# The down product of a fused block: token tiles grouped 2, 3, 3 in place of 3, 3, 2

## The chip, the cores and the metric

One core of one Trainium2 chip runs one program. The metric is the device time of one execution, in microseconds (us). The kernel before takes 1655.97 us, the median of three runs (1651.63 to 1657.54).

## What is computed

The reference applies three residual blocks to x, 1024 tokens (16 x 64) of 1024 features: cross attention against a context of 1601 positions, a gated feed-forward block whose hidden values are thinned by rank, and a routed low-rank layer with 8 experts of rank 16. The second block is the one that matters here:

```python
s = silu(x @ w_gate.T)                      # 1024 x 2752
s[the 1376 smallest of |s| in each row] = 0
x = x + (s * (x @ w_up.T)) @ w_down.T        # x is normalised before both products
```

## The kernel before

The program runs attention (`attention_fast`), the feed-forward block (`ffn_fast`, lines 997 to 1602), the routed layer (`mixture`) and a check, each behind a barrier of all engines. The change lies in `ffn_fast`.

The 1024 tokens are eight tiles of 128 tokens. Weights and activations of a product are split in a high and a low part, and each product is the sum of three matmuls (high by high, high by low, low by high). `ffn_fast` computes the gate product into DRAM (`s`), then the up product, transposed, into DRAM (`u_t`). Beside the up product VectorE (DVE) and ScalarE (ACT) search the threshold of each row, tile by tile, and DVE writes the thinned rows to DRAM (`sk`). Four tiles are thinned by then. The thinning of tiles 4 to 7 is interleaved with the down product, by step number: `FINISH_AT = {0: 4, 4: 5, 24: 6, 28: 7}` starts the last four passes of a tile (`nearest`, `best`, `choose`, `keep`, L1358 to L1391) in four steps one after another, and from step 9 (`LATE_ROUNDS_AT`) every second step up to 21 has one round of the search for tiles 6 and 7 (`search`, L1321 to L1350; `compare` on ACT). On the SP queue `LATE_SK_AT = {5: 4, 9: 5, 28: 6, 32: 7}` names the step at which a thinned tile is stored and the row data of the next one is loaded.

The down product takes the tokens in three groups (`GROUPS`), since three tiles by 1024 output features fill six PSUM banks and the transposes need the other two. For each group it runs over the 2752 hidden values in 22 chunks of 128 (the last has 64), so there are 66 steps, n = 0 to 65, and w_down is read and split anew for each group. A step n, for a group of m tiles, is:

- SP: `load_down(n + 2)` waits until POOL is done with the low part of n, and loads a 128 x 1024 chunk of w_down (L1179). `load_turn(n + 3)` then loads m tiles of `sk` (L1169) and of `u_t` (L1172). SP takes these, the stores of thinned tiles and the loads for them in one order.
- GpSimd (POOL): `d_hi` (a cast, L1277) once the matmuls of n - 2 are done, then `d_lo` (L1279). Their size does not depend on m.
- TensorE (PE): `turn(n + 2)`, m transposes (L1578), then `down(n)`, m x 3 x 2 matmuls of 128x512 (L1595).
- DVE: `multiply(n)` (L1416), m x 128 wide, reads the transposes; `take_low(n - 1)` (L1425), as wide, reads two SBUF tiles; then whatever thinning the step has. ACT makes `h_hi` (L1507) between the two.

At the third step of a group DVE adds x to the finished output of the group before (`add_in`, L1433, two operations for each tile). The first product of a group waits for these, tile by tile. At the fourth step SP stores those tiles (L1190), waits for the stores to land, and loads the x of the group now being computed (L1185). The last group's `add_in` and stores stand at the end.

```python
for i in range(len(GROUPS[gi])):
    for a, (hp, wp) in enumerate(((h_hi, d_hi), (h_hi, d_lo), (h_lo, d_hi))):
        for o in range(2):
            last = pe.matmul(bank[2 * i + o][:, :], ...)
```

Of the kernel before, what the change touches and what calls it, by code (L numbers as in the profile page):

```python
# [629 lines left out]
def attention_fast(nc, x, ctx_nat, ctx_t, mask, x1, outside):  # L630
# [3 lines left out]
    with ExitStack() as ctx:  # L634
# [6 lines left out]
        PER = TC  # L641
        GROUPS = B * PER
        UNITS = 2 * B
# [106 lines left out]
        def _(pool):  # L750
            identity(pool, eye[:, :], eye_ready)
            pool.memset(ones[:, :], 1.0).then_inc(ones_ready, 1)
            for g in range(GROUPS):
                if g % PER == LAST:
# [9 lines left out]
        def _(dve):  # L764
# [35 lines left out]
            def add_mask(g, hp):  # L800
                p = g % PER
                h = 2 * g + hp
                r = rows(p)
                if hp == 0:
                    dve.wait_ge(scores_ready, g + 1)
                if h >= SLOTS:
                    dve.wait_ge(exp_done, h + 1 - SLOTS)
                c0, c1 = (c for _, c in parts(p))
                if p == LAST:
                    m = mask_t[0:r, c0].rearrange("p k s -> p (k s)").unsqueeze(1).broadcast_to([r, 4, 256])  # L810
                    into = masked[0:r, h % SLOTS, :].rearrange("p (n q) -> p n q", n=4)
                    of = scores[0:r, h % SLOTS].rearrange("p h (c q) -> p (h c) q", c=2)
                else:
                    m = mask_t[0:r, c0:c1 + 1].rearrange("p c k s -> p (c k s)").unsqueeze(1).broadcast_to([r, 2, 512])
                    into = masked[0:r, h % SLOTS, :].rearrange("p (h n) -> p h n", h=2)
                    of = scores[0:r, h % SLOTS]
                dve.tensor_tensor(into, of, m, ALU.add).then_inc(mask_added, 1)  # L817
# [18 lines left out]

            for g in range(GROUPS + 8):
                if g < GROUPS:
                    add_mask(g, 0)
# [19 lines left out]
        def _(act):  # L859
# [11 lines left out]
            def exponential(g, hp):  # L871
                p = g % PER
                h = 2 * g + hp
                r = rows(p)
                act.wait_ge(mask_added, h + 1)
                if g >= RING and hp == 0:
                    act.wait_ge(pv_done, g + 1 - RING)
                    act.wait_ge(paired, pairs_before(g + 1 - RING))
                act.activation(probs[0:r, g % RING, hp * HALF:(hp + 1) * HALF], masked[0:r, h % SLOTS, :],  # L879
                               ACT.Exp).then_inc(exp_done, 1)  # L880
# [7 lines left out]
            act.wait_ge(mask_turned, 1)  # L888
            for g in range(GROUPS + 4):
                if g < GROUPS:  # L890
                    exponential(g, 0)
# [103 lines left out]
def ffn_fast(nc, x1, w_gate, w_up_t, w_down, s, sk, u_t, x2, settled):  # L995
# [3 lines left out]
    with ExitStack() as ctx:  # L999
# [2 lines left out]
        START, SLOPE, WINDOW = 0.755, 5.3e-4, 4  # L1002
        AIM = float(KEEP_OUT + WINDOW - 1)
        PAIRS = TILES // 2
        GROUPS = ((0, 1, 2), (3, 4, 5), (6, 7))
        STEPS = len(GROUPS) * IC
        MAGS, TURNS, HS, OUTS = 3, 4, 3, 4
        GBANKS = 6
# [1347 lines left out]
def program(nc, x, ctx_nat, ctx_t, mask, w_gate, w_up, w_up_t, w_down, router_wt, router_b, a_t, b_t, out):  # L2356
    qstack = nc.dram_tensor("qstack", [B, 3 * HD, NH * S], F32, kind="Internal").ap()
    shifts = nc.dram_tensor("shifts", [2, 2, HALF_Q], F32, kind="Internal").ap()
    x1 = nc.dram_tensor("x1", [TOK, D], F32, kind="Internal").ap()
    x2 = nc.dram_tensor("x2", [TOK, D], F32, kind="Internal").ap()  # L2360
    s = nc.dram_tensor("s", [TOK, I], F32, kind="Internal").ap()
    u = nc.dram_tensor("u", [TOK, I], F32, kind="Internal").ap()
    sk = nc.dram_tensor("sk", [TOK, I], F32, kind="Internal").ap()
    u_t = nc.dram_tensor("u_t", [I, TOK], F32, kind="Internal").ap()
    with nc.sbuf_tensor("outside", [P, 1], F32) as outside, nc.sbuf_tensor("settled", [P, TILES], F32) as settled, \
            nc.sbuf_tensor("all_bad", [HD, 1], I32) as all_bad:
        attention_fast(nc, x, ctx_nat, ctx_t, mask, x1, outside[:, :])
        ffn_fast(nc, x1, w_gate, w_up_t, w_down, s, sk, u_t, x2, settled)
        mixture(nc, "mix", x2, router_wt, router_b, a_t, b_t, out)
        verdict(nc, outside[:, :], settled[:, :], all_bad[:, :])  # L2370
        bad = nc.values_load(all_bad[0:1, 0:1], min_val=0, max_val=4 * P)
        with nc.If(bad > 0):
            anew(nc, x, ctx_nat, ctx_t, mask, w_gate, w_up, w_down, router_wt, router_b, a_t, b_t, out,
                 qstack, shifts, x1, x2, s, u)
# [36 lines left out]
```

## Time and profile before

| what | value |
|---|---|
| median of three runs | 1655.97 us |
| the profiled execution | 1656.46 us |
| its span, first to last instruction | 1654.8 us |
| PE busy | 1418.1 us (86%) |
| DVE busy | 1052.4 us (64%) |
| POOL busy | 856.0 us (52%) |
| mean granted TensorE clock | 0.95 of full speed |
| first product of the down stage to its last | 1189.9 to 1542.3 us |

Busy time counts the time in which an engine has an instruction under way. The profile gives for each idle stretch of an engine what ended it. Where an instruction waits for several semaphores, the one that came last by the profile is named. Times in the trace are counted from the start of the span. A matmul row's duration overlaps the next row's, since matmuls are pipelined; the distance between starts is the pace.

### The profile page before, as it was taken

How to read it: one execution, taken by the hardware profiler on the slowest of the kernel's cores; microseconds unless marked ns; L12 is line 12 of the kernel's file. 1: busy time of each engine (PE TensorE's matmuls, PEld its weight loads, DVE VectorE, ACT ScalarE, POOL GpSimd, SP SyncE). 2: the span in 40 equal slices, each digit the busy share in tenths (PEclk: the TensorE clock that was granted, in tenths of full speed). 3: DMA queues.
4: the chain of work that ended last, by engine and by line, in shares of the span. 5: the costliest groups of instructions: out<-in, count | busy, mean ns of one | idle time of the engine just before them, and what ended most of it. 6: DMA issues, size and time to landing. Idle time of an engine off the chain costs nothing. (4 is left out here: it accounts for less than half of the span.)

```text
span 1654.8 us, 30061 instructions
## 1 busy us (share of the span) xinstructions
PE 1418.1 (86%) x12775; PEld 1040.1 (63%) x12775; DVE 1052.4 (64%) x1381; ACT 661.1 (40%) x773; POOL 856.0 (52%) x411
## 2 busy tenths in 40 slices
PE   3899998999999996699999999998878888968365
PEld 3455554545555553699999988886666666756262
DVE  7788888888988886810000099987378894324243
ACT  2677777777777774121111253333113200100020
POOL 0677877777777875422232233333365656768200
PEclk9999999999999998799999999999999999989688
DMA  7033322222232301312313455564476566566402
GB/s 270 15 107 102 113 81 94 81 94 81 94 121 97 121 25 42 142 69 83 123 69 108 167 163 196 195 247 130 162 245 215 162 230 243 178 201 198 163 0 104
DMA packets 125568, 220.62 MB, mean 133 GB/s; under 512 B 10017, under 2 KB 96113, under 8 KB 121329
## 3 DMA queue, kind: packets, MB, share of 16 engines
q1 hardware_dynamic: 123200, 217.53, 38.5%
q8 instruction: 102, 1.67, 0.4%
q10 hardware_dynamic: 2224, 1.08, 0.2%
q14 instruction: 42, 0.34, 0.1%
HBM read 172.18 MB, written 46.40 MB: 132 GB/s over the span
## 5 line engine op out<-in xcount | busy, mean ns | idle before, releaser
L761 POOL TENSOR_TENSOR fast_pair<-fast_probs 128x1024 f32<-128x1024 f32 x192 | 463.1, 2412 | 183.4 <-ACT fast_probs L879 105.4
L817 DVE TENSOR_TENSOR fast_masked<-fast_scores,fast_mask_t 128x1024 f32<-128x1024 f32 (+1 forms) x416 | 489.7, 1218 | 71.7 <-PE fast_scores L937 65.4
L879 ACT ACTIVATE fast_probs<-fast_masked 128x1024 f32<-128x1024 f32 (+1 forms) x416 | 440.1, 1058 | 144.4 <-DVE fast_masked L817 130.1
L937 PE MATMUL fast_scores<-fast_qT,fast_kraw 32*128 32x256 f32 (+1 forms) x3328 | 242.9, 406 | 46.6 <-DVE fast_masked L817 45.9
L937 PEld LDWEIGHTS fast_scores<-fast_qT,fast_kraw 32*128 32x128 f32 (+1 forms) x3328 | 150.8, 184 | 135.1 <-DVE fast_masked L817 94.6
L954 PE MATMUL fast_o_acc<-fast_probs,fast_vraw 128*32 128x256 f32 (+1 forms) x3328 | 227.6, 388 | 1.7 <-ACT fast_probs L879 1.7
L1279 POOL TENSOR_TENSOR ffn_d_lo<-ffn_d_raw,ffn_d_hi 128x1024 fp32r<-128x1024 f32 x66 | 166.7, 2526 | 5.3
L1542 PE MATMUL ffn_bank<-ffn_g_hi,ffn_z_hi 128*128 128x344 f32 x512 | 166.2, 325 | 2.6 <-ACT ffn_res L1476 2.6
L1542 PE MATMUL ffn_bank<-ffn_g_lo,ffn_z_hi 128*128 128x344 f32 x512 | 165.0, 322 | 0.0
L1542 PE MATMUL ffn_bank<-ffn_g_hi,ffn_z_lo 128*128 128x344 f32 x512 | 164.8, 322 | 0.0
L1310 DVE TENSOR_SCALAR ffn_cut<-ffn_total 128x2 f32<-128x2 f32 x4 | 2.9, 717 | 246.4 <-ACT ffn_mag L1480 246.4
L954 PEld LDWEIGHTS fast_o_acc<-fast_probs,fast_vraw 128*32 128x32 f32 (+1 forms) x3328 | 87.4, 109 | 109.2 <-ACT fast_probs L879 54.2
L1595 PE MATMUL ffn_bank<-ffn_d_hi,ffn_h_hi 128*128 128x512 f32 (+1 forms) x352 | 123.0, 432 | 34.5 <-DVE ffn_h_lo L1425 19.6
L1507 ACT CAST ffn_h_hi<-ffn_t_h 128x384 fp32r<-128x384 f32 (+1 forms) x66 | 31.4, 478 | 285.4 <-DVE ffn_t_h L1416 285.4
L1565 PE MATMUL ffn_bank<-ffn_z_hi,ffn_u_hi 128*128 128x512 f32 (+1 forms) x352 | 138.5, 393 | 7.0 <-POOL ffn_u_lo L1267 6.5
L1277 POOL CAST ffn_d_hi<-ffn_d_raw 128x1024 fp32r<-128x1024 f32 x66 | 76.9, 1166 | 127.4 <-PE ffn_bank L1595 89.1
L1565 PE MATMUL ffn_bank<-ffn_z_lo,ffn_u_hi 128*128 128x512 f32 (+1 forms) x352 | 137.8, 391 | 0.0
L1565 PE MATMUL ffn_bank<-ffn_z_hi,ffn_u_lo 128*128 128x512 f32 (+1 forms) x352 | 137.7, 391 | 0.0
L1416 DVE TENSOR_TENSOR ffn_t_h<-ffn_bank,ffn_t_u 128x384 f32<-128x384 f32 (+1 forms) x66 | 33.6, 510 | 148.8 <-PE ffn_bank L1578 147.9
L1265 POOL CAST ffn_u_hi<-ffn_u_raw 128x1024 fp32r<-128x1024 f32 (+1 forms) x22 | 24.6, 1118 | 189.6 <-PE ffn_bank L1565 106.1
L973 PE MATMUL fast_o_acc<-fast_pair,fast_ones 128*32 128x256 f32 x1536 | 118.1, 379 | 0.9 <-POOL fast_pair L761 0.9
L1595 PE MATMUL ffn_bank<-ffn_d_lo,ffn_h_hi 128*128 128x512 f32 (+1 forms) x352 | 115.7, 411 | 0.0
(154 smaller groups left out, 2003.6 us busy)
## 6 DMA issues: line engine op xcount, KB each, us to landing
ffn_d_raw<-w_down SPq DMA_DIRECT2D x63, 512.0 KB, 3.7
fast_kraw<-ctx_t SPq DMA_DIRECT2D x32, 800.5 KB, 5.8
fast_vraw<-ctx_nat SPq DMA_DIRECT2D x16, 1536.0 KB
ffn_g_raw<-w_gate SPq DMA_DIRECT2D x8, 1376.0 KB, 8.9
s<-ffn_res SPq DMA_DIRECT2D x8, 1376.0 KB, 6.1
ffn_mag<-s SPq DMA_DIRECT2D x8, 1376.0 KB, 10.2
ffn_sx<-s SPq DMA_DIRECT2D x8, 1376.0 KB, 6.0
sk<-ffn_sx SPq DMA_DIRECT2D x8, 1376.0 KB, 6.9
```

Of the source, the lines that this page charges most:

```text
L761: pool.tensor_tensor(pair[:, n % PAIRS], both[:, :, 0, :], both[:, :, 1, :], ALU.add).then_inc(paired, 1)
L817: dve.tensor_tensor(into, of, m, ALU.add).then_inc(mask_added, 1)
L879: act.activation(probs[0:r, g % RING, hp * HALF:(hp + 1) * HALF], masked[0:r, h % SLOTS, :], ACT.Exp).then_inc(exp_done, 1)
L937: last = pe.matmul(scores[0:r, (2 * g + h // 2) % SLOTS, h % 2, i * 256:(i + 1) * 256], kraw[q, b % BUFS, u, c * P:c * P + r], qT[q, b, u, ...
L954: last = pe.matmul(o_acc[q, u, 0:256], vraw[0:r, b % BUFS, c, u * P + h * HD:u * P + (h + 1) * HD], probs[0:r, g % RING, (2 * h + i) * 256 ...
L973: last = pe.matmul(o_acc[h * HD:(h + 1) * HD, u, 256:512], ones[:, :], pair[:, n % PAIRS, h, :], start=False, stop=final, skip_group_check ...
L1277: pool.tensor_copy(d_hi[j][0:r, :], d_raw[j][0:r, :]).then_inc(d_hi_done, 1)
L1279: pool.tensor_tensor(d_lo[j][0:r, :], d_raw[j][0:r, :], d_hi[j][0:r, :].bitcast(F32), ALU.subtract).then_inc(d_lo_done, 1)
L1416: dve.tensor_tensor(t_h[n % 2][0:r, 0:w], bank[6 + n % 2][0:r, 0:w], t_u[n % TURNS][0:r, 0:w], ALU.mult).then_inc(h_ready, 1)
L1542: last = pe.matmul(bank[i % GBANKS][:, 0:NJ], zp[:, k, ts], wp[n % 2][:, k, :], start=(k == 0 and a == 0), stop=(k == DK - 1 and a == 2))
L1565: last = pe.matmul(bank[i % 4][0:r, :], wp[f % 2][:, k, 0:r], zp[:, k, gs], start=(k == 0 and a == 0), stop=(k == DK - 1 and a == 2))
L1595: last = pe.matmul(bank[2 * i + o][:, :], hp[jh][0:r, ts], wp[j][0:r, o * 512:(o + 1) * 512], start=(k == 0 and a == 0), stop=(k == IC - 1 ...
```

## The change

```diff
-        GROUPS = ((0, 1, 2), (3, 4, 5), (6, 7))
+        GROUPS = ((0, 1), (2, 3, 4), (5, 6, 7))
```

The step numbers of all interleaved work stay as they are. Steps 0 to 21 now have two tiles in place of three, steps 22 to 43 have three as before, and steps 44 to 65 have three in place of two. The chunk loads of w_down and POOL's split are the same 66. The first group loads two tiles of x, the last three. The number of matmuls and transposes in all is unchanged. The two boundaries between groups store two and three tiles of output, where they stored three and three, and the end stores three where it stored two.

## Rows read from the trace of the kernel before

**Rows 1.** The page: the span.

```profile
span 1654.8 us, 30061 instructions
```

**Rows 2.** Stretches of the down product: length, busy time of each engine, granted clock, DMA.

```profile
core 0: us, PE busy (x) PEld busy (x) DVE busy (x) ACT busy (x) POOL busy (x), PEclk, DMA share, GB/s
1189.80:1251.80 62.00, 47.70 (x189) 36.69 (x190) 51.90 (x58) 9.69 (x13) 36.76 (x18) 0.89 0.69 242
1251.80:1318.20 66.40, 58.75 (x253) 46.84 (x253) 55.95 (x95) 19.09 (x22) 40.38 (x24) 0.94 0.55 174
...
1189.80:1325.50 135.70, 111.30 (x463) 87.09 (x463) 112.81 (x159) 29.80 (x37) 81.98 (x44) 0.92 0.62 206
1325.50:1445.60 120.10, 104.31 (x459) 82.89 (x459) 68.85 (x83) 10.97 (x22) 80.83 (x45) 0.94 0.66 222
1445.60:1542.30 96.70, 75.54 (x302) 56.27 (x302) 33.47 (x43) 7.75 (x19) 70.95 (x41) 0.90 0.55 176
1397.80:1438.40 40.60, 40.27 (x189) 32.44 (x187) 11.66 (x18) 4.52 (x9) 31.28 (x17) 1.00 0.59 182
1479.70:1532.30 52.60, 42.95 (x184) 31.85 (x182) 20.31 (x26) 5.31 (x13) 45.96 (x27) 0.97 0.60 183
```

**Rows 3.** Who waited for whom: PE, in the first group (1189.8 to 1325.5).

```profile
PE ffn_bank L1595 <- DVE ffn_h_lo L1425: 15.8, 7, 4.7
```

**Rows 4.** The same view of PE in the last group (1445.6 to 1542.3).

```profile
PE ffn_bank L1578 <- DMA ffn_t_u<-u_t: 18.8, 13, 8.6
```

**Rows 5.** Groups of instructions on DVE in the first group: busy, mean ns, idle before.

```profile
L1425 DVE TENSOR_TENSOR ffn_h_lo<-ffn_t_h,ffn_h_hi 128x384 fp32r<-128x384 f32 x23 | 27.8, 1209 | 4.7 <-ACT ffn_h_hi L1507 4.7
L1321 DVE TENSOR_SCALAR_CACHE_REDUCE ffn_below<-ffn_mag,ffn_cut 128x2752 bf16<-128x2752 f32 x8 | 24.6, 3071 | 0.1
L1416 DVE TENSOR_TENSOR ffn_t_h<-ffn_bank,ffn_t_u 128x384 f32<-128x384 f32 x22 | 12.2, 553 | 11.5 <-PE ffn_bank L1578 10.7
```

**Rows 6.** Groups of instructions on DVE and POOL in the last group.

```profile
L1425 DVE TENSOR_TENSOR ffn_h_lo<-ffn_t_h,ffn_h_hi 128x256 fp32r<-128x256 f32 x19 | 22.3, 1175 | 0.0
L1416 DVE TENSOR_TENSOR ffn_t_h<-ffn_bank,ffn_t_u 128x256 f32<-128x256 f32 x18 | 7.6, 424 | 53.6 <-PE ffn_bank L1578 53.6
...
L1279 POOL TENSOR_TENSOR ffn_d_lo<-ffn_d_raw,ffn_d_hi 128x1024 fp32r<-128x1024 f32 x20 | 49.1, 2453 | 1.6
L1277 POOL CAST ffn_d_hi<-ffn_d_raw 128x1024 fp32r<-128x1024 f32 x19 | 20.1, 1059 | 21.1 <-PE ffn_bank L1595 12.1 <-DMA ffn_d_raw<-w_down 8.7
```

**Rows 7.** Timeline of PE: start, length, two matmuls to a row.

```profile
1191.78 1.05 PE L1595 MATMUL ffn_bank<-ffn_d_hi,ffn_h_lo 128*128 128x512 f32 x2
1192.63 1.05 PE L1595 MATMUL ffn_bank<-ffn_d_hi,ffn_h_hi 128*128 128x512 f32 x2
...
1294.60 0.62 PE L1595 MATMUL ffn_bank<-ffn_d_lo,ffn_h_hi 128*128 128x512 f32 x2
1295.06 0.62 PE L1595 MATMUL ffn_bank<-ffn_d_hi,ffn_h_lo 128*128 128x512 f32 x2
```

**Rows 8.** Timeline of DVE in the first group, steps 7, 8 and 16.

```profile
1231.82 3.08 DVE L1391 SCALAR_TENSOR_TENSOR ffn_sx<-ffn_near,ffn_thr,ffn_sx 128x2752 f32<-128x2752 f32 x1 [4.64 <-DMA ffn_sx<-s]
...
1241.55 0.75 DVE L1425 TENSOR_TENSOR ffn_h_lo<-ffn_t_h,ffn_h_hi 128x384 fp32r<-128x384 f32 x1 [4.65 <-ACT ffn_h_hi L1507]
...
1287.08 0.55 DVE L1425 TENSOR_TENSOR ffn_h_lo<-ffn_t_h,ffn_h_hi 128x384 fp32r<-128x384 f32 x1
```

**Rows 9.** Timeline of the SP queue: a thinned tile stored, the next loaded.

```profile
1218.78 0.43 SPq L1157 DMA_DIRECT2D sk<-ffn_sx  x1
...
1225.70 0.33 SPq L1153 DMA_DIRECT2D ffn_sx<-s  x1
```

**Rows 10.** Timeline of SP and PE at the second boundary of groups.

```profile
1459.69 1.81 SPq L1190 DMA_DIRECT2D x<-ffn_xin  x3
1466.47 0.81 SPq L1185 DMA_DIRECT2D ffn_xin<-x  x2
...
1474.52 0.69 PE L1578 MATMUL ffn_bank<-ffn_eye,ffn_t_sk 128*128 128x128 f32 x2 [8.64 <-DMA ffn_t_u<-u_t]
```

**Rows 11.** Timeline of DVE at the end of the down product.

```profile
1542.43 2.48 DVE L1433 TENSOR_TENSOR ffn_xin<-ffn_bank,ffn_xin 128x512 f32<-128x512 f32 x4 [6.53 <-PE ffn_bank L1595]
```

## The prediction

> **What bounds the kernel now.** I read the page first, then the stretches of the down product, one for each group of token tiles, and then the waits of PE in each. The span is 1654.8 us [rows 1]; the part that the change can reach is the down product, and in it each group has 22 steps. The three groups take 135.7, 120.1 and 96.7 us [rows 2], so 6.17, 5.46 and 4.40 us for a step. The reader should see that the two groups of three tiles have the same matmuls and differ by 15.6 us.
>
> Where nothing disturbs it, a step of three tiles takes 40.6 / 9 = 4.51 us, with PE busy for 40.27 of 40.60 us at the full granted clock [rows 2]: it is bound by PE. An undisturbed step of two tiles takes 52.6 / 13 = 4.05 us [rows 2]. Two matmuls start 0.46 us apart for the pair [rows 7], so a step's 12 matmuls are 2.76 us and a third is saved on PE, but only 0.46 us in the step. The rest is idle: POOL's two operations are 2.45 and 1.06 us, 3.5 us together [rows 6], whatever the number of tiles, and PE waits 18.8 us for the loads in front of the transposes [rows 4]. Those loads are issued behind the w_down load, which waits for POOL.
>
> The first group has another bound. DVE is busy for 112.81 of 135.70 us there, against 33.47 of 96.70 in the last [rows 2], since it finishes tiles 4 and 5 and searches for tiles 6 and 7. PE waits 15.8 us for its `h_lo` [rows 3]. So now three-tile steps stand where DVE limits, and two-tile steps where PE would be the limit. The change turns that round. What it brings is what the first group gives up less what the last one takes on.
>
> **First group, three tiles to two.** I take it in three stretches.
>
> Steps 0 to 8 last 62.0 us, with DVE busy for 51.9 [rows 2]. Nearly all of its idle time is two waits: 4.64 us for the row data of tile 5 and 4.65 us for ACT, which stood before `h_hi` in its own order until the rows of tile 7 had landed [rows 8]. Both come from SP: it stored tile 4 at 1218.78 and could issue the next load only at 1225.70 [rows 9], and the store stood behind the w_down load of step 7, so behind POOL at step 5, so behind the matmuls of step 3. With six matmuls less in each step the store can go up to about 6 us earlier. DVE itself saves 0.553 - 0.424 = 0.13 us in each multiply [rows 5, 6], 1.2 us in nine steps. I take 5.5 us.
>
> Steps 9 to 20 are six pairs in 66.4 us, 11.07 us a pair; DVE is busy for 55.95, 9.33 us a pair [rows 2]. The biggest single operation is the 3.07 us count of each round [rows 5], and it does not shrink. The idle 1.74 us is largely the wait of the multiply for the transposes, 10.7 us in the whole group [rows 5]: these stand on PE behind `down(n - 3)`, which gets 6 x 0.23 = 1.4 us shorter. A pair should then be DVE's 9.33 less 0.26 for two narrower multiplies, plus some 0.35 of gaps between dependent operations and an estimated 0.5 of blocking by a denser POOL, about 9.95 us. That is 1.1 us by six pairs, 6.7 us.
>
> Step 21 and the boundary lose one short product, 1.4 us; I take 1.3. **First group: -13.5 us.** Its ends: only the multiply gets cheaper, 22 x 0.13 = -3 us; or DVE is never idle, 112.8 - 2.9 = 110, that is -26 us.
>
> At this place the clock speaks against the change. After an idle stretch a pair of matmuls starts 0.85 us after the one before, later 0.46 us [rows 7]; these are the two levels 1.2 and 2.4 GHz, and the granted clock of the first stretch is 0.89 of full [rows 2]. Twelve matmuls at the low level cost 6 x 0.39 = 2.3 us more. With less work between waits PE will restart low more often. It had room: 9.95 us of a pair against 5.5 us of matmuls, so I cost it at nothing. If a pair starts low twice, the chain through the transposes holds DVE for about 1 us of it, 6 us in all, and this is in the end of -3. The Trainium skill, "TensorE: Matmul & The Clock Gate", section "HAM oscillation — how this bites in real kernels", says that work too thin to cover its waits is throttled anew each time. By that rule the pairs would gain about nothing, and the sum would be slower by 6 us.
>
> **Second group, three tiles as before.** Its work keeps its step numbers. The boundary has two additions of 0.62 us less [rows 11], in a stretch where DVE goes on to finish tile 6, and a store less ahead of SP's wait for the stores. **-2 us**, between 0 and -4.
>
> **Last group, two tiles to three.** It takes 96.7 us. I build it from steps: the first one starts after an idle stretch and is at the low clock for most of it, 5.9 us; 20 at 4.5, 90 us; one more that restarts low behind the stall for x, 5.8; and the stall. Now SP issues three stores at 1459.69, waits for them to 1466.47, then loads x and only then the next chunks, and the transposes come at 1474.52 after 8.64 us idle [rows 10]. Three-tile steps give 3 x 0.6 = 1.9 us more cover until then, and the third load of x takes some of it back: I take 8.2 us. Sum 5.9 + 90 + 5.8 + 8.2 = 109.9. **+13 us.** The ends: 22 x 0.46 = +10 from the undisturbed steps alone, and +16 if the extra x load and two restarts come on top.
>
> **The end.** Two additions more after the last matmul, 2 x 0.62 us [rows 11], with the third store behind them, and the barrier behind that: **+1.3 us**, between 1.2 and 2. Nothing covers it. The start of the group loads one tile of x less, hidden under the first multiply. The order of stored tiles is no new wait: group two now needs tile 4 and not tile 5, the last needs tile 7 as before.
>
> **The sum**: -13.5 - 2 + 13 + 1.3 = -1.2 us against the profiled 1656.46, 1655.3 us. The median of the runs shown stands 0.5 us lower, so I forecast 1655 us. A measurement of this kernel can tell about 0.5%, 8.3 us, from no change: below 1647.7 is faster, above 1664.3 slower.
>
> **The rivals.**
>
> 1. *DVE comes free* (faster). In the first group the search and finish work runs back to back, SP's stores move up, and the two 4.6 us waits vanish. For it: DVE is idle for 22.9 us there, nearly all in waits that begin on PE or SP. The group falls by 22 to 26 and not 13.5, the sum is -12, 1644 us. Against it: these waits hang on one another, and the store and load of a tile, 7 us to the load's issue [rows 9], don't get shorter. Chance 0.28.
>
> 2. *POOL and DVE block each other* (slower). The undisturbed `h_lo` is 0.55 us at 384 columns [rows 8], but its mean is 1.21 in the first group and still 1.18 at 256 columns in the last [rows 5, 6]. So it is mostly waiting, and narrowing it brings nothing. POOL's 3.5 us a step is fixed; the shorter the step, the more of it falls on DVE's small dependent operations of a round. If that takes another 1 to 1.5 us in a pair, the first group gains only 3 to 4 us, and the last still costs 13: 1665 us. It decides from the point where blocking grows by more than 0.8 us a pair. The Trainium skill, "SBUF — State Buffer", section "SBUF: two separate sides", has it that a DVE operation with two SBUF inputs and a GpSimd one exclude each other for a whole instruction; the rows on `h_lo` agree. Chance 0.17 (with a longer x stall in the last group).
>
> 3. *The trade is even*, my forecast: 0.55. Its own range is 1648 to 1664.
>
> That the change doesn't do what it says can be left aside: the group list sets every loop of the stage.
>
> **The numbers.** Faster by over 0.5%: 0.28; within: 0.55; slower by over 0.5%: 0.17. The ends of the terms added would give 1628 to 1674; both extremes at once are not likely, and the range of 1643 to 1666 leaves about 2 in 10 out.
>
> **What would show it.** In the new profile the first group should last about 122 us with DVE busy over 85% of it, the pairs of steps 9 to 20 some 10 us each, the store of tile 4 about 5 us earlier. The second should be near 118. The last should be near 110, with steps of 4.5 us, PE at the full clock and one stall of about 8 us. Wrong would be: a first group at 110 or below (rival 1) or above 130, with `h_lo` and the small operations of the search at over 2 us (rival 2); two-tile steps starting low in every pair; a stall for x in the last group of over 12 us.

## The result, and the profile after

The changed kernel takes 1674.84 us (median of four runs, 1668.26 to 1679.56); the kernel before took 1656.76 in the runs beside it. The ratio is 1.0104, with a 95% interval of 1.0054 to 1.0155. A second set of six runs (below, e17) gave 1.0135 (1.0110 to 1.0161). So the change costs 1.0 to 1.4%, some 20 us. The forecast was 1655 with a range of 1643 to 1666: the time lies above it.

The profiled execution took 1668.26 us, with a span of 1666.1, the shortest of the four. It answers to [rows 1, 2] with these stretches of the down product: steps 0 to 8, 9 to 20, the rest of the first group, then the three groups, and at last thirteen undisturbed steps.

```profile
span 1666.1 us, 30061 instructions
...
1190.70:1246.00 55.30, 36.61 (x126) 26.82 (x126) 47.96 (x57) 8.70 (x13) 34.00 (x17) 0.82 0.64 225
1246.00:1313.50 67.50, 46.41 (x170) 35.44 (x171) 62.27 (x95) 17.92 (x23) 42.26 (x26) 0.82 0.49 159
1313.50:1322.30 8.80, 4.33 (x16) 2.78 (x16) 6.99 (x7) 1.03 (x2) 5.50 (x3) 0.64 0.67 213
1190.70:1322.30 131.60, 87.35 (x312) 65.04 (x312) 117.21 (x158) 27.64 (x37) 81.76 (x44) 0.81 0.57 191
1322.30:1444.50 122.20, 104.97 (x463) 83.61 (x463) 71.44 (x81) 11.28 (x22) 79.21 (x44) 0.94 0.65 217
1444.50:1558.10 113.60, 102.31 (x453) 82.00 (x453) 30.96 (x43) 9.76 (x19) 72.54 (x41) 0.94 0.53 175
1484.80:1545.40 60.60, 58.46 (x277) 47.27 (x275) 18.19 (x26) 6.68 (x13) 46.73 (x26) 1.00 0.57 179
```

The columns are those of [rows 2]: length, busy time of PE, its weight loads, DVE, ACT and POOL, granted clock. The groups go from 135.7, 120.1 and 96.7 us to 131.6, 122.2 and 113.6: -4.1, +2.1 and +16.9. With 0.9 us more ahead of them and 4.5 less behind, that is the 11.3 us between the spans. The 4.5 us are not the change's. Its own part of the end, six additions in place of four, is longer; what became shorter is the routed layer behind it, which with the additions in front of it takes between 108 and 114 us in the kernels run here, none of which touches it. The profiled executions are 12 us apart and the medians 18: the profile accounts for the 12, and no profile shows where the other 6 lie.

DVE has narrower operations in the first group, and yet its busy time rose from 112.8 to 117.2 us. By operation, in steps 9 to 20 of the changed kernel:

```profile
L1321 DVE TENSOR_SCALAR_CACHE_REDUCE ffn_below<-ffn_mag,ffn_cut 128x2752 bf16<-128x2752 f32 x7 | 21.5, 3070 | 0.0
L1425 DVE TENSOR_TENSOR ffn_h_lo<-ffn_t_h,ffn_h_hi 128x256 fp32r<-128x256 f32 x11 | 12.3, 1117 | 0.0
...
L1337 DVE TENSOR_TENSOR ffn_da<-ffn_off 128x2 f32<-128x2 f32 x5 | 3.0, 596 | 0.0
L1346 DVE TENSOR_TENSOR ffn_db<-ffn_off 128x2 f32<-128x2 f32 x5 | 2.9, 584 | 0.0
L1350 DVE TENSOR_TENSOR ffn_cut<-ffn_cut,ffn_da 128x2 f32<-128x2 f32 x5 | 2.3, 464 | 0.2
...
L1336 DVE TENSOR_TENSOR ffn_db<-ffn_cut 128x2 f32<-128x2 f32 x5 | 0.8, 167 | 0.2
```

The kernel before has in its own steps 9 to 20:

```profile
L1425 DVE TENSOR_TENSOR ffn_h_lo<-ffn_t_h,ffn_h_hi 128x384 fp32r<-128x384 f32 x11 | 12.0, 1092 | 0.0
...
L1336 DVE TENSOR_TENSOR ffn_db<-ffn_cut 128x2 f32<-128x2 f32 x5 | 4.1, 812 | 0.2
...
L1350 DVE TENSOR_TENSOR ffn_cut<-ffn_cut,ffn_da 128x2 f32<-128x2 f32 x5 | 0.8, 161 | 0.2
...
L1346 DVE TENSOR_TENSOR ffn_db<-ffn_off 128x2 f32<-128x2 f32 x5 | 0.8, 152 | 0.0
L1337 DVE TENSOR_TENSOR ffn_da<-ffn_off 128x2 f32<-128x2 f32 x5 | 0.7, 150 | 0.0
```

`h_lo` is a third narrower and takes as long as before. Of the operations on two elements a partition the first three shown are about three to four times as long; one, L1336, went the other way, from 4.1 to 0.8 us. All the small operations of the rounds together, without the counts, rose from 17.4 to 25.2 us. What they wait for stands in the timelines of DVE and of POOL in the changed kernel, step 12:

```profile
1263.54 2.36 DVE L1339 SCALAR_TENSOR_TENSOR ffn_da<-ffn_da 128x2 f32<-128x2 f32 x1
...
1266.13 0.74 DVE L1343 TENSOR_TENSOR ffn_da<-ffn_da,ffn_db 128x2 f32<-128x2 f32 x1
...
1266.98 2.31 DVE L1346 TENSOR_TENSOR ffn_db<-ffn_off 128x2 f32<-128x2 f32 x1
...
1270.04 0.41 DVE L1425 TENSOR_TENSOR ffn_h_lo<-ffn_t_h,ffn_h_hi 128x256 fp32r<-128x256 f32 x1
```

```profile
1263.50 2.38 POOL L1279 TENSOR_TENSOR ffn_d_lo<-ffn_d_raw,ffn_d_hi 128x1024 fp32r<-128x1024 f32 x1
1265.82 1.04 POOL L1277 CAST ffn_d_hi<-ffn_d_raw 128x1024 fp32r<-128x1024 f32 x1
1266.94 2.34 POOL L1279 TENSOR_TENSOR ffn_d_lo<-ffn_d_raw,ffn_d_hi 128x1024 fp32r<-128x1024 f32 x1
```

Each of the two long DVE operations begins within 0.04 us of a `d_lo` and ends with it. The one between them, 0.74 us where 0.16 is usual, ends with the cast. `h_lo`, with no `d_lo` left to meet, takes 0.41 us. The same holds through the first groups of both kernels: each small operation of a round that ran more than 0.2 us over its shortest ended with an operation of POOL, or its own length behind one, and so did each long `h_lo`.

A second hold-up is on SP, at step 10. The rows are SP's store of a thinned tile, its load of the next one 6.38 us later, and PE:

```profile
1242.14 0.43 SPq L1157 DMA_DIRECT2D sk<-ffn_sx  x1
1248.52 0.33 SPq L1153 DMA_DIRECT2D ffn_sx<-s  x1
...
1257.12 0.69 PE L1578 MATMUL ffn_bank<-ffn_eye,ffn_t_sk 128*128 128x128 f32 x2 [4.69 <-DMA ffn_t_u<-u_t]
```

In the last group the stall for x answers to [rows 10], and the additions at the end to [rows 11]:

```profile
1467.33 1.28 SPq L1185 DMA_DIRECT2D ffn_xin<-x  x3
...
1477.45 0.90 PE L1578 MATMUL ffn_bank<-ffn_eye,ffn_t_sk 128*128 128x128 f32 x3 [9.14 <-DMA ffn_t_u<-u_t]
...
1558.22 3.68 DVE L1433 TENSOR_TENSOR ffn_xin<-ffn_bank,ffn_xin 128x512 f32<-128x512 f32 x6 [8.70 <-PE ffn_bank L1595]
```

### The profile page after: what moved, and what is told of

Read it like the earlier page. It is cut to its first block and busy times, and to the rows that moved or that the text cites. A ratio compares the mean times of both kernels' runs of the same rounds, so it can differ in the third digit from the quotient of the medians.

```text
span 1666.1 us, 30061 instructions
## 1 busy us (share of the span) xinstructions
PE 1418.7 (85%) x12775; PEld 1041.8 (63%) x12775; DVE 1059.8 (64%) x1381; ACT 661.1 (40%) x773; POOL 856.1 (51%) x411
## 5 line engine op out<-in xcount | busy, mean ns | idle before, releaser
L1279 POOL TENSOR_TENSOR ffn_d_lo<-ffn_d_raw,ffn_d_hi 128x1024 fp32r<-128x1024 f32 x66 | 171.4, 2597 | 5.3
L1277 POOL CAST ffn_d_hi<-ffn_d_raw 128x1024 fp32r<-128x1024 f32 x66 | 72.0, 1092 | 140.8 <-PE ffn_bank L1595 97.5
L1595 PE MATMUL ffn_bank<-ffn_d_lo,ffn_h_hi 128*128 128x512 f32 (+1 forms) x352 | 117.0, 415 | 0.0
```

The source lines that it names most:

```text
L1277: pool.tensor_copy(d_hi[j][0:r, :], d_raw[j][0:r, :]).then_inc(d_hi_done, 1)
L1279: pool.tensor_tensor(d_lo[j][0:r, :], d_raw[j][0:r, :], d_hi[j][0:r, :].bitcast(F32), ALU.subtract).then_inc(d_lo_done, 1)
L1595: last = pe.matmul(bank[2 * i + o][:, :], hp[jh][0:r, ts], wp[j][0:r, o * 512:(o + 1) * 512], start=(k == 0 and a == 0), stop=(k == IC - 1 ...
```

## The experiments

Four explanations were open. A: in the first group DVE's chain sets the time, and POOL blocking DVE takes what narrower work saves. B: PE, restarting at the low clock, sets it. C: the length of PE's step does. D: SP waits for a stored tile in front of the loads of the next steps. The rows shown for an experiment are those of its groups, in the columns above. Ratios are to the kernel before, with its 95% interval.

**The x loads moved, on both orders (e1, e2).**

```diff
                 if gi >= 1 and k == 3:
                     store_x(gi - 1)
+                if gi >= 1 and k == 12:
                     load_x(gi)
```

> The kernel before (groups of 3, 3, 2), with the loads of x moved from the fourth step of a group to its thirteenth; the stores stay. If the stall of 8.64 us in the last group comes from SP waiting for the stores in front of the w_down and transposed loads, it disappears, the step behind it starts at the full clock, and the last group goes from 96.7 to about 86 us; the second group, whose stall is 2.06 us behind a DVE wait, gains 2 to 5 us. Sum -12 us (ratio 0.993). If the stall comes from the traffic of stores and loads itself, it moves with the loads and the time stays within 3 us.

> The changed kernel (2, 3, 3) with the same move of the x loads. If SP's wait is the cause: the stall of 9.14 us and the slow step behind it go, the last group falls from 113.6 to about 102 us, and the time is 12 us under the changed kernel, about 1662 (ratio 1.003 to before). The difference from the same edit on 3, 3, 2 then stays near 17 us: the x stall is no part of the difference. If the third x tile is what made the last group dearer than forecast, the difference between the two falls by 3 us or more.

Measured: 0.9981 (0.9961 to 1.0) on 3, 3, 2, and 1.0123 (1.0083 to 1.0162) on 2, 3, 3. The last group, in the one and in the other:

```profile
1443.00:1534.00 91.00, 74.00 (x302) 54.77 (x302) 36.95 (x43) 7.73 (x19) 70.46 (x41) 0.94 0.58 187
```

```profile
1449.60:1558.20 108.60, 101.89 (x453) 81.01 (x453) 32.72 (x43) 9.76 (x19) 72.47 (x41) 0.97 0.57 183
```

Each last group is 5 to 6 us shorter than in the kernel that it was edited from, half of what was expected: PE's longest wait for the loads is 3.8 and 3.5 us and no longer 8.6 and 9.1. The whole gains less, 0.2% on 3, 3, 2 and nothing that can be told on 2, 3, 3: the second groups, which were to gain 2 to 5 us, lasted 124.0 and 124.6 us, against 120.1 and 122.2. The difference of the last groups is still 17.6 us, so the stall for x is no part of the change's loss that shows.

**More work for PE, and a lighter POOL (e3, e4).** In e3 the first group does the second tile's product twice.

```diff
-                for i in range(len(GROUPS[gi])):
+                for i in range(3):
...
-                    ts = slice(i * P, (i + 1) * P)
+                    it = min(i, len(GROUPS[gi]) - 1)
+                    ts = slice(it * P, (it + 1) * P)
```

> The changed kernel, with six more matmuls in each step of the first group, into the two PSUM banks that it leaves free (the second tile's product once more, results unused): PE does the work of three tiles while DVE stays at two. Theory A, DVE sets the time of the first group and the mutual blocking of DVE and POOL took what the narrower work saved: the first group stays at 132 us within 3, DVE busy near 117 us. Theory B, PE restarting at the low clock sets it: PE is busier, the mean clock there rises from 0.81 to 0.9, and as the extra matmuls are done at the full clock the group stays or falls, with the waits for h_lo (29.5 us) halved. If PE's length of a step does set the time (theory C), the group grows by 10 us or more.

Measured: 1.0164 (1.0137 to 1.0192). The first group:

```profile
1184.80:1323.30 138.50, 112.54 (x443) 88.01 (x443) 106.96 (x158) 27.65 (x37) 80.77 (x44) 0.88 0.55 179
```

The clock rose from 0.81 to 0.88 and PE's waits for `h_lo` fell from 29.5 to 12.4 us, both as B had it, and the group grew all the same, by 6.9 us; against the second profile of the changed kernel (e17, below) the growth is 2.3. So the faster clock did not shorten the group, but the run adds work too and cannot price the clock by itself. PE's length counts (C), but 132 more matmuls at 0.23 us are 30 us, of which a quarter shows at most. DVE's busy time fell to 107, so neither is A in its plain form enough: PE and DVE wait for one another in turn. And 138.5 is no less than the 135.7 of three tiles: the narrower DVE work alone brings nothing that shows here.

In e4 the cast of w_down goes from POOL to ACT.

```diff
             for n in range(STEPS):
                 take_high(n)
+                down_high(n)
                 if n == LATE_ABS_AT:
```

> The changed kernel with the cast of w_down (d_hi) moved from POOL to ACT, in the order after h_hi of the same step. POOL then has 2.45 us in a step and not 3.5. Theory A (blocking): DVE's busy time in the first group falls by 3 to 6 us (from 117.2), the group by 4 to 8. Theory B (low clock): DVE's time falls but PE's restarts stay, the group stays within 3 us. The last two groups stay within 2 us, since PE bounds them, unless ACT's own order delays h_hi: then they grow.

Measured: 1.0099 (1.0068 to 1.0129). DVE's busy time in the first group fell to 85 us, much further than expected, and the group lasted 133.9 us, no less than before the edit. New waits stand in its place: DVE for ACT's count of the search, which now stood behind the cast, 20.5 us, and PE for the transposed loads, 22.8 us. Busy time was no measure of the path.

**POOL's work taken out of the first group (e6, e7).**

```diff
-                j, r = n % 2, rows(n % IC)
+                j, r, w = n % 2, rows(n % IC), 128 if 2 <= n < IC else D
...
-                pool.tensor_copy(d_hi[j][0:r, :], d_raw[j][0:r, :])
+                pool.tensor_copy(d_hi[j][0:r, 0:w], d_raw[j][0:r, 0:w])
```

> The changed kernel (2, 3, 3), with POOL's cast and subtraction of w_down done on 128 of the 1024 columns in steps 2 to 21 (the rest of the split weights there is left from steps 0 and 1, so the first group's output is not the down product). POOL neither blocks DVE nor paces PE in the first group. Theory A (blocking): the operations of DVE that took over 2 us fall to their free length, DVE's busy time goes from 117 to about 82 us and the first group from 132 to 115 or less. Theory B (low clock and the ring of PE and DVE): DVE's busy time falls as much, but the group stays over 125 us. Theory D, SP's wait for the stored tile in front of the next step's loads: the waits of PE for the transposed loads, 10.2 us, stay or grow.

> The kernel before (3, 3, 2), with the same narrow POOL work in steps 2 to 21. Theory A: its first group falls too, from 135.5, but PE's 18 matmuls in a step hold it near 115 to 120 (22 x 4.5 = 99 and the waits for the search); the first group of 2, 3, 3 is then shorter by 8 us or more, which is the gain that I forecast. Theory B: both stay above 125 and within 4 us of each other.

Measured: 0.9996 (0.9975 to 1.0017) on 2, 3, 3 and 0.9909 (0.9883 to 0.9935) on 3, 3, 2. The first groups:

```profile
1183.10:1292.30 109.20, 82.03 (x312) 62.58 (x312) 81.23 (x158) 27.64 (x37) 29.91 (x44) 0.83 0.69 230
```

```profile
1189.70:1310.30 120.60, 105.33 (x463) 84.77 (x463) 82.73 (x158) 29.81 (x37) 25.13 (x44) 0.92 0.69 231
```

Steps 9 to 20, in the one and in the other:

```profile
1231.80:1281.50 49.70, 40.17 (x171) 31.57 (x171) 40.82 (x95) 17.91 (x23) 11.90 (x24) 0.93 0.75 241
```

```profile
1242.70:1303.00 60.30, 55.27 (x254) 45.01 (x253) 42.12 (x94) 19.09 (x22) 9.74 (x25) 0.97 0.69 224
```

This settles what took the first group's gain. With so little work on POOL the group of two tiles is 11.4 us shorter than the group of three; with POOL's full work it was 4.1 in the profile above and nothing in the repeat (e17). In steps 9 to 20 it is 10.6 us shorter, where the change had made it 1.1 longer (67.5 against 66.4), and the small operations of the rounds take 9.6 us in all and not 25.2. POOL's work had cost DVE 36 and 30 us of busy time, and the short steps more than the long ones (22.4 against 15.1 us for the group).

Two other ways in which POOL could act went with its work. That PE waits for `d_lo` itself is not the cause: in the changed kernel these waits are 5.3 us in the first group, none of them in steps 9 to 20. What the loads behind POOL cost by way of SP is not separated. SP's own waits stayed, as D had it: PE waits 14.6 us for the transposed loads in e6, and 10.2 in the changed kernel.

The order 2, 3, 3 still loses, 1652.3 against 1641.3 us. The last groups are as they were, 113.9 and 95.0 us, and the second group of e6 lasts 127.6 us against 121.2 in e7, for which no run shows the cause.

**SP's wait for stored tiles (e10, e11).**

```diff
-                    if t + 1 < TILES:
+                    if n == 5:
                         load_sx(t + 1)
+                if n in (12, 30):
+                    load_sx({12: 6, 30: 7}[n])
```

> The changed kernel with x loaded at the thirteenth step of a group, and the row data of tiles 6 and 7 loaded at steps 12 and 30 in place of 9 and 28, so that SP does not wait about 7 us for the store of the tile before in front of the loads of the steps. Theory D: the 4.69 us wait of PE at step 10 and the 6.29 us at step 29 go, the first two groups fall by 4 to 6 us each, and the time is 8 to 12 us under that of the x move alone (1673), ratio near 1.006. Theory A: the wait is only covered by DVE's chain, the first group stays within 3 us.

> The same two moves on groups of 3, 3, 2. The wait at step 29 goes (5.46 us and the slow step behind it), that at step 12 is small there. Theory D: 5 to 7 us under the x move alone (1652), ratio near 0.994; the first group stays at 134. If SP's wait hurts the short steps more than the long ones, this gains less than the same edit on 2, 3, 3.

Measured: 1.0070 (1.0045 to 1.0094) on 2, 3, 3, down from 1.0123 with the x move alone; 0.9999 (0.9975 to 1.0023) on 3, 3, 2, no gain over its 0.9981. The first group of 2, 3, 3 falls from 133.5 to 128.3 us, that of 3, 3, 2, at 135.3, does not fall. D holds for the short steps: the wait of PE at step 10 is gone (the longest for these loads in the group is 1.4 us), and the time moved the way it should, while nothing is gained where a step is long enough to cover SP's wait. The size, 5 us, is read from one profile of each and is hardly larger than the 4.6 us between two profiles of one kernel (e17). The second groups did not fall (123.8, 125.1), against the expectation.

**The cast on ACT behind its count (e9).**

```diff
                 if 0 <= r < ROUNDS - 1 and off_beat == 0:
                     compare(PAIRS - 1, r)
+                down_high(n)
```

> The changed kernel with the cast of w_down on ACT, as in the run before with this cast, but behind ACT's count of the search (compare) and not in front of it. In that run DVE's busy time fell by 32 us and yet the group stayed at 133.9, while DVE waited 20.5 us for ACT's count. Theory A (blocking by POOL): with the count no longer behind the cast, these 20.5 us go and the first group falls to about 120 us; the whole to about 1660. Theory B (ring of PE and DVE at the low clock): DVE waits for PE in their place, the group stays above 128.

Measured: 1.0082 (1.0063 to 1.0102). The first group is 130.4 and not 120, but it divides in two. Steps 13 to 20, in this kernel and in the changed one:

```profile
1276.60:1311.80 35.20, 28.98 (x114) 21.28 (x114) 30.24 (x60) 19.24 (x23) 19.18 (x8) 0.91 0.58 175
```

```profile
1270.60:1313.50 42.90, 31.85 (x114) 24.23 (x115) 41.42 (x61) 11.11 (x14) 25.45 (x16) 0.83 0.41 125
```

There it is 7.7 us shorter, DVE is busy 11 us less, and `h_lo`, which here never meets an operation of POOL, is at its free length:

```profile
L1424 DVE TENSOR_TENSOR ffn_h_lo<-ffn_t_h,ffn_h_hi 128x256 fp32r<-128x256 f32 x7 | 2.9, 415 | 0.0
```

Ahead of that a wait came in that I had not thought of. ACT, in its order, waits for the rows of tile 7 with the casts of the next steps behind it, and PE behind those:

```profile
1234.35 2.50 ACT L1479 ACTIVATE ffn_mag<-ffn_mag 128x2752 f32<-128x2752 f32 x1 [13.98 <-DMA ffn_mag<-s]
...
1240.44 0.79 PE L1602 MATMUL ffn_bank<-ffn_d_hi,ffn_h_hi 128*128 128x512 f32 x1 [9.01 <-POOL ffn_d_lo L1278]
```

**Two tiles in the middle (e8).**

```diff
-        GROUPS = ((0, 1, 2), (3, 4, 5), (6, 7))
+        GROUPS = ((0, 1, 2), (3, 4), (5, 6, 7))
```

> Groups of 3, 2, 3. The first group keeps the three tiles of the kernel before and should last 135 us, the last takes the three tiles of the changed kernel and should last 113.6. If the dearer last group is the larger part of the change's loss, this stands in the open with what two tiles save in the middle, where DVE has only the finishing of tiles 6 and 7: the middle group falls from 120 to about 107 (22 times 0.46 and the stall for x unchanged). Sum: +17 - 13, about +4 us, ratio 1.002. If short steps are held up by DVE or SP there too, the middle falls by 5 or less and the ratio is 1.007.

Measured: 1.0047 (1.0024 to 1.0069). The groups are 135.7, 117.0 and 114.3 us. The last one is as dear as in 2, 3, 3 behind a first group like that of before, so its price doesn't depend on what goes ahead. The middle gained 3.1 us, not 13: short steps are held up there as well, though DVE is busy for only 73 of 117 us. What holds them is the loads: PE waits for those in front of the transposes 13 times, 23.7 us in all.

**The edits together (e14, e13, e15, e16, e18).** e14 is 3, 3, 2 with the x move and e9's cast; e13 is 2, 3, 3 with both and the later loads of e10. e15 (3, 3, 2) adds to e14, and e16 (2, 3, 3) to e13,

```diff
-        LATE_MAG_AT, LATE_ABS_AT, LATE_ROUNDS_AT = 6, 7, 9
+        LATE_MAG_AT, LATE_ABS_AT, LATE_ROUNDS_AT = 4, 7, 9
```

so that the rows of tile 7 are loaded two steps earlier. e18 has this line and the x move alone, on 3, 3, 2.

> The kernel before (3, 3, 2) with the cast on ACT behind its count, and x loaded at the thirteenth step of a group. POOL has 2.45 us in a step: the first group should fall from 134 to 126 or less as blocking shrinks; the two-tile steps of the last group, whose loads wait for POOL, should fall from 4.05 to about 3.6 us, so the group from 91 to about 83. Sum with the x move about 1638 us, ratio 0.99. If ACT's order delays h_hi, the three-tile steps grow over 4.5 us and there is no gain.

> Groups of 2, 3, 3 with the cast on ACT behind its count, x loaded at the thirteenth step, and the row data of tiles 6 and 7 at steps 12 and 30. If POOL's blocking and SP's order were all that stood against short steps under the search, the first group falls to about 112 us, the second to 118, the last stays at 108: about 1645 us, ratio 0.994. It should still be no better than 3, 3, 2 with the cast and the x move, since its last group is 20 us longer.

> Groups of 2, 3, 3 with the cast on ACT, x loaded at the thirteenth step, the row data of tiles 6 and 7 at steps 12 and 30, and the rows of tile 7 loaded at step 4 in place of 6. If the waits of SP and ACT were what was left, the 9 us wait of PE at steps 7 and 8 goes and the first group falls from 124.8 to about 115 us: 1649 us, ratio 0.996. If the load at step 4 only delays the store and load of tile 5 behind it, the wait moves there and the group stays at 122 to 125.

> Groups of 3, 3, 2 with the cast on ACT, x at the thirteenth step, and the rows of tile 7 at step 4. The wait of PE behind POOL (8.6 us) in the first group goes, the group falls from 136 to about 128 us, the last stays at 90.5: about 1641 us, ratio 0.991, and better than 2, 3, 3 with the same edits by 8 us, the last group's 15 us less what the first is longer.

> Groups of 3, 3, 2 with the cast on POOL as before, x at the thirteenth step and the rows of tile 7 at step 4. The 4.65 us in which DVE waits for h_hi behind ACT's wait for these rows goes: 3 to 5 us less than with the x move alone, ratio 0.996; within 0.001 of 0.998 if the wait moves to the row data of tile 5.

Measured: e14 0.9966 (0.9944 to 0.9987), e13 1.0020 (1.0000 to 1.0040), e16 0.9969 (0.9947 to 0.9992), e15 0.9946 (0.9922 to 0.9970), e18 1.0006 (0.9983 to 1.0030). The three groups of e16, then of e15:

```profile
1189.50:1306.70 117.20, 84.03 (x312) 61.66 (x312) 95.80 (x158) 49.02 (x59) 56.05 (x23) 0.85 0.66 217
1306.70:1428.50 121.80, 105.98 (x462) 83.80 (x462) 61.28 (x81) 32.95 (x44) 55.21 (x22) 0.93 0.66 218
1428.50:1535.00 106.50, 101.17 (x453) 81.18 (x453) 28.51 (x43) 29.27 (x39) 49.07 (x21) 0.97 0.57 186
```

```profile
1183.70:1315.80 132.10, 108.42 (x463) 85.34 (x463) 95.31 (x158) 51.66 (x59) 57.88 (x23) 0.90 0.64 211
1315.80:1435.50 119.70, 105.38 (x459) 83.48 (x459) 61.28 (x83) 32.67 (x44) 56.85 (x23) 0.93 0.68 222
1435.50:1527.30 91.80, 74.20 (x302) 55.42 (x302) 34.92 (x43) 27.94 (x39) 49.38 (x21) 0.93 0.59 186
```

With the cast off POOL and the three waits moved, a complete kernel has its first group of two tiles at 117.2 us, 14.9 under that of three in e15, and its last group 14.7 over. By these profiles the trade of the first group for the last is even. In the medians it is not: e16 takes 1647.93 us and e15 1642.91, and their twelve and nine runs put the difference at 5 us, give or take 3.

Nor do the two kernels have the same edits. e15 lacks the later loads of e10, and its first group keeps the wait that e16 has lost. PE's waits there:

```profile
PE ffn_bank L1586 <- DMA ffn_t_u<-u_t: 18.9, 4, 7.7
```

The wait of 7.7 us stands at step 10, behind a store and load of SP that are 6.84 us apart. The order 3, 3, 2 with all four edits was not run, so 14.9 us is likely more than two tiles are worth.

e15 is the fastest of the complete kernels and beats both that the document began with; its last group gained nothing from the cast (91.8 us, and 91.0 with the x move alone), nor did e14's (90.5), against the expectation of 83. The earlier load by itself brings nothing (e18).

**The changed kernel again (e17).**

> The changed kernel once more, unchanged. Ratio to before between 1.009 and 1.012, the profiled run's three groups within 3 us of 131.6, 122.2 and 113.6.

Measured: 1.0135 (1.0110 to 1.0161), the ratio just above what I had written. Its groups are 136.2, 124.7 and 111.3 us: the first is 4.6 us longer than in the first profile, beyond the 3 us expected, and the last 2.3 shorter. Steps 0 to 8 are the same, 55.4 us; the difference lies in steps 9 to 20 (70.0 us) and in step 21 (10.8). So one profile's group length is good to within some 5 us in this stage, and the first group's gain of 4.1 is not told from nothing.

## Why the prediction was wrong

*What bounds the kernel.* Right: DVE in the first group, and PE's steps in the undisturbed ones. But of the 112.81 us in which DVE was busy there, which the forecast took for its load, some 30 were time under POOL's block, as e7 shows.

*First group, -13.5 us*: the step that failed. It measured -4.1 us in one profile and +0.5 in the other, on three stretches.

Steps 0 to 8 went from 62.0 to 55.3 us, 6.7 for the 5.5 forecast, but in part by luck. The store of tile 4 came about 2 us earlier after the group's start (1217.41 against 1218.78 in the trace, with a start 0.9 us later) and not 5 to 6. The two waits behind it fell from 4.64 to 2.3 us and from 4.65 to 4.2, 2.8 in all. The rest is DVE's busy time, 3.9 us less, of which the multiplies are 1.2.

Steps 9 to 20 were to fall by 6.7 us and grew by 1.1. The term at fault is the "estimated 0.5 of blocking by a denser POOL" in a pair. DVE's busy time rose by 6.3 us where the narrower multiplies had taken off 1.6, so the blocking grew by 7.9 us in six pairs, 1.3 us a pair. That is 4.9 us of the 7.8 by which this stretch was missed. e6 and e7 show that POOL is the cause: without its work two tiles save 10.6 us in these steps. The small operations of a round, each dependent on the one before, can each meet a `d_lo`. I had the rows for it and gave it half a microsecond. The other 3.1 us are idle time of DVE, 5.2 us where the sum had 2.1. The SP wait at step 10, which keeps PE idle for 4.69 us and which long steps had covered, was not priced at all; without it e10's group is some 5 us shorter than e2's, hardly more than the spread of single profiles.

The end stretch (step 21 and the boundary) was to lose 1.3 us and gained 1.5. DVE came to the additions 7.3 us after the start of step 21, behind two `h_lo` of 2.07 and 2.60 us, where it had taken 5.9, and PE waited 4.46 us for them and not 2.45.

*The clock at that place* was put at nothing, and the runs bound it without giving its price. The group's clock fell from 0.92 to 0.81. The Trainium skill, "TensorE: Matmul & The Clock Gate", section "HAM oscillation — how this bites in real kernels", says that work too thin to cover its waits is throttled anew each time, and the fall agrees with that. But in steps 9 to 20 DVE was busy for 62.27 of 67.50 us, so with the same blocking a faster PE could have given back at most the other 5.2 us, and in e3 a higher clock brought no shorter group. In e6 the same steps ran at 0.93, and in e16 at 0.91, against 0.82: the clock rose together with the gain there, and what part of the gain it made is not shown. What that rule would give, pairs that gain nothing, is what was measured, but the blocked operations are a cause that it does not have.

*Second group, -2 us*: measured +2.1 and +4.6. Two additions and a store less were there (SP's wait for the stores was 6.15 us), and PE's wait of 3.8 us for `h_lo` stayed. Of the 2.1 us, 0.8 are PE's longest wait for the transposed loads (6.29 against 5.46 us); the rest is spread over single steps, and why it came was not tried.

*Last group, +13 us*: measured +16.9 and +14.6, mis-sized, and in the first profile a microsecond outside the bounds. The undisturbed step was 60.6 / 13 = 4.66 us, not 4.5 (single late loads), the stall 9.14 us and not 8.2, and the step behind it 6.9 us and not 5.8.

*The end, +1.3 us*: the six additions took 3.68 against 2.48 us, +1.2. The 4.5 us less behind the last group, which hid part of the loss in the profile, were in no term.

*The sum* had two large terms of opposite sign; one lost its cover. The profile came out 12.5 us over it: 9.4 in the first group, 4.1 in the second, 3.9 in the last, and 4.9 less ahead and behind. The blocking beyond its half microsecond is the largest single cause and less than half of the whole. The medians are 6 us further apart than the profiles: both profiled executions of the changed kernel were the shortest of their series, and no profile shows those 6 us.

Rival 2, POOL and DVE block each other, is what happened, at a chance of 0.17. Its 1665 us came close to the profiled 1668, partly by luck: blocking of 1 to 1.5 us more in a pair takes 6 to 9 us from the gain of 13.5, which leaves 4.5 to 7.5 and not "3 to 4", and at its deciding point of 0.8 us the time would still have been within 0.5% of the kernel before. The rule of the Trainium skill that it names ("SBUF — State Buffer", section "SBUF: two separate sides") agrees with the runs: in e9 `h_lo` is at 0.415 us where it meets no operation of POOL. The ends of the terms, added as they stand, give 1637 to 1671 us and not 1628 to 1674; the measured median lies above either.

## What to carry to other kernels

A step whose size is cut gets shorter only if everything of fixed size in it does too: here POOL's 3.5 us and SP's 6 to 7 us waits had been covered, for the most part, by long steps, and came out when the steps were short. Price the cover, not only the work. A busy share can be waiting: where an operation on two elements takes 2.3 us, look at what the neighbour engine has under way, and in a chain of dependent small operations count a possible block for each. And where two orders of the same work are compared, free both of the same hold-ups: 2, 3, 3 lost 1.0 to 1.4% as it stood, and 0.3% with the cast moved and the waits taken out (e16 against e15, which kept one of them). Last, take a second profile of the same kernel before a difference of 4 us in a stage is believed: here it was gone in the second.

## What had not been expected of the hardware

Moving a 1.04 us cast from POOL to ACT, where it takes 1.045 us, took 32 us off DVE's busy time in 22 steps (e4), more than the 24 us that its 22 casts take in all. POOL's other operation met DVE less often too: three of the twenty narrow `h_lo` ran long in e4 and eleven in the changed kernel, and of the small operations of the rounds only the very last (1.30 us). Why the two fell apart like that is not shown. With the cast behind the count (e9) it was 17 us.

The count of a round, 3.07 us over 2752 columns with an accumulated result, took between 3.06 and 3.09 us in all 32 cases of each profile, and the multiply, which reads PSUM and SBUF, never over 0.56 us. `h_lo`, with both inputs in SBUF, took from 0.41 us to 2.8, and operations on one to eight elements a partition up to 2.4 us. Two inputs are not needed for it: L1325, which adds a constant to two elements a partition, took 2.23 us in the changed kernel, to the end of a `d_lo`, 3.21 in its second run, past a `d_lo` to the end of the cast behind it, and 0.17 in the kernel before, while its like on one element a partition (L1328, L1330) never took over 0.16.
